# VectorE's step in another order: both gain products together, adapter work behind evictions, raw down weight fetched earlier

## The chip, the cores and the metric

The kernel runs on one core of a Trainium2 chip. The metric is the device time of one execution in microseconds (us), median over runs. One program does both layers of the reference, one after the other.

## The reference

Two layers of the same form follow each other. In each, every item of a batch of 128 (128 rows by 1024) picks one of three adapters: layer 0 by the item's own number, layer 1 by its own set of weights and the same number.

```
h = x @ W_down[r] + b_down[r]        # 1024 -> 512
h = gelu(h)
u = h @ W_up[r] + b_up[r]            # 512 -> 1024
y = x + u
y = (y - mean(y)) * rsqrt(var(y) + 1e-5)
x = y * gamma[r] + beta[r]
```

## The kernel before

**Pairs and steps.** The items are sorted by adapter (`c_ord`), so that neighbours share one, and taken two at a time. There are 65 pairs for each layer (`NP`), 130 in all (`NPH`); the second layer reads what the first has stored in `mid`. A step is the time of one pair. TensorE, VectorE, ScalarE and GpSimd each have a list of work for a step, written out by hand. The pairs overlap: in step i TensorE multiplies the down product of pair i and the up product of pair u = i-3, VectorE also transposes and splits the hidden values of pair w = i-2, and scales pair u-1.

**Accuracy.** Every fp32 operand is split in a high part (fp32r, made by ScalarE with a copy) and a low part (made by VectorE with a subtraction); a product is three matmuls of 128x128 by 128x512. A down product of a pair is 48 matmuls. The up product of two items takes seven products instead of eight (a Strassen scheme), six matmuls each, 42 in all. So a step is 90 matmuls.

**TensorE's order in a step** (`step` in its block): product 0 into bank `bX`, a quarter of the first item's down product, product 1 into `bZ`, a quarter, product 2 into `bX`, a quarter, and so on to product 6, then two quarters of the second item's. Products alternate between the banks `bX` and `bZ`. After a product VectorE adds the bank to the rows `xt` in SBUF: `onto` 1 to 3 (L834), `last_onto` 4 to 7 (L842, which also sums). Product n+1 needs the eviction of product n-1, since it goes on in that bank: product 4 waits for onto 3, product 5 for last_onto 4, product 6 for last_onto 5, and product 2 of the next step for onto 1 of that step. These are counts of the semaphore `s_v`.

**VectorE's order in a step** is given by two functions, `begin` and `end`. `end` of step i is run, then `begin` of step i+1. After `end` come the transposes of the hidden values, `transpose_h` (L809), in `begin`. In `end`, `scale` (L865) does (x - mean) * gamma for each of the two items of pair u-1; `transpose_x` (L795, in layer 1 only) turns blocks of x; `low_x` (L802), `low_h` (L824) make low parts. ScalarE then multiplies the scaled rows by the reciprocal deviation (`normal`, L633) and GpSimd adds beta (`shift`, L415), after it has raised the variance to -1/2 and multiplied it (`norm`, L405 and L408).

**Loops.** Of the steps of each layer most run in a hardware loop of six steps a turn (`steps`, `M = 6`). VectorE's and ScalarE's loop is closed between `begin` and `end`, just before onto 3.

**Change of adapter.** `when_new` reads a flag from SBUF to a register (L221) and branches; the work behind it is done when a pair has another adapter than the one before: once at the start, once in each layer and once between the layers, four times in all. `take_wd_0`, `take_wd_1`, `take_wu_0`, `take_wu_1`, `take_wu_2` split the raw weights, the high part on ScalarE and the low part on VectorE; `factors` makes the sums of blocks of the up weight that the scheme needs (L749, L751), and `take_wu_1` two more (L770, L772). Each of these operations on 128x1024 values is one VectorE instruction. `ready(p, s)` tells TensorE that the weights of a pair are there. SyncE issues all DMAs from one list; it waits in line for each.

## Time and profile before

| | |
|---|---|
| median of 3 runs | 2804.37 us (2803.05 to 2805.55) |
| the profiled execution's own time | 2803.86 us |
| its span, first to last instruction | 2802.0 us |
| mean granted clock of TensorE | 0.987 |
| TensorE busy | 2700.2 us, 96% of the span, 11714 matmuls |
| VectorE busy | 2194.5 us, 78% |
| ScalarE busy | 1702.5 us, 61% |
| GpSimd busy | 1344.6 us, 48% |

Busy time counts overlapping matmuls once. The profiled execution is 0.5 us under the median; 1.9 us of its time lie outside the span.

### The profile page before, as it was taken

To read this page: it belongs to the slowest core of one execution; us is meant where nothing else is said; L and a number is where in the kernel's file an instruction comes from. 1 tells how busy PE (TensorE), PEld (TensorE's weight loads), DVE (VectorE), ACT (ScalarE), POOL (GpSimd) and SP (SyncE) were. 2 spreads that over 40 slices of the span, in tenths; PEclk is the share of its full clock that TensorE was granted. 3 is DMA by queue.
4 is the path that set the end of the run, shared out by engine and by line. 5 is a ranking of instruction groups with operands and counts; after the bars stand their busy time and mean duration, and the time that the engine had idled before them with its cause. 6 is when DMAs were issued, how large, how long until landed. Compare 5 with 4: busy or idle time off the path is not lost.

```text
span 2802.0 us, 57328 instructions
## 1 busy us (share of the span) xinstructions
PE 2700.2 (96%) x11714; PEld 2208.4 (79%) x11714; DVE 2194.5 (78%) x3341; ACT 1702.5 (61%) x2907; POOL 1344.6 (48%) x1050
## 2 busy tenths in 40 slices
PE   6999999999999999999989999999889999999997
PEld 5788888877788888888778787878667887878785
DVE  4777776768777776777898888888888888888886
ACT  4566665666666665656656566656555566666564
POOL 0455555544555555555444444444434444444446
PEclk9999999999999999999999999999999999999998
DMA  6665666666665666666776665666676665666664
GB/s 189 199 209 199 212 209 207 212 218 219 204 223 199 212 209 207 208 204 211 217 223 202 192 222 190 214 198 201 198 210 204 211 204 189 214 201 204 197 202 145
DMA packets 365915, 573.60 MB, mean 205 GB/s; under 512 B 40960, under 2 KB 240768, under 8 KB 365440
## 3 DMA queue, kind: packets, MB, share of 16 engines
q1 hardware_dynamic: 365440, 569.61, 62.9%
q14 instruction: 463, 3.79, 0.5%
q8 instruction: 12, 0.20, 0.0%
HBM read 364.97 MB, written 204.47 MB: 203 GB/s over the span
## 4 chain that ended last, share of the span: by engine, by line
PE 73%; issue 9%; DVE 9%; DVEq 2%; ACT 2%; DMA 2%; SPq 1%; POOL 1%; ACTq 0%; POOLq 0%
PE pD L463 38%; PE bX L475 20%; PE bZ L475 15%; DVE xt L842 2%; DVEq L221 2%; DMA cbd<-in_bd 1%; DVE hl L824 1%; DVE xt L865 1%; DVE wul L743 1%; ACT pC L625 1%; DVE xl L802 1%; DVE xt L834 1%; DVE xT L795 1%; ACT xh L573 1%; SPq L269 0%
## 5 line engine op out<-in xcount | busy, mean ns | idle before, releaser
L415 POOL TENSOR_TENSOR xt<-xt,cgb 128x1024 f32<-128x1024 f32 x260 | 649.7, 2500 | 419.5 <-ACT xt L633 419.5
L463 PE MATMUL pD<-wdh,xh 128*128 128x512 f32 x2080 | 814.3, 392 | 11.1 <-ACT pD L588 10.4
L463 PE MATMUL pD<-wdl,xh 128*128 128x512 f32 x2080 | 813.2, 391 | 0.0
L463 PE MATMUL pD<-wdh,xl 128*128 128x512 f32 x2080 | 812.6, 391 | 0.0
L633 ACT ACTIVATE xt<-xt,rstd 128x1024 f32<-128x1024 f32 x260 | 298.8, 1150 | 459.2 <-POOL rstd L408 380.8
L463 PEld LDWEIGHTS pD<-wdh,xh 128*128 128x128 f32 x2080 | 393.3, 189 | 95.2 <-issue 11.2
L865 DVE SCALAR_TENSOR_TENSOR xt<-xt,nmean,cgb 128x1024 f32<-128x1024 f32 x260 | 462.3, 1778 | 0.8 <-POOLq L435 0.8
L463 PEld LDWEIGHTS pD<-wdl,xh 128*128 128x128 f32 x2080 | 393.3, 189 | 82.0
L463 PEld LDWEIGHTS pD<-wdh,xl 128*128 128x128 f32 x2080 | 392.8, 189 | 82.4
L475 PE MATMUL bX<-wuh,hh 128*128 128x512 f32 x1040 | 412.2, 396 | 45.7 <-DVE xt L834 22.4
L625 ACT ACTIVATE pC<-xt,nmean 128x512 f32<-128x512 f32 x520 | 359.8, 692 | 137.8 <-DVE nmean L850 73.4
L423 POOL TENSOR_TENSOR cs<-hT 128x256 f32<-128x256 f32 x130 | 96.6, 743 | 650.7 <-DVE hT L809 650.7
L475 PE MATMUL bX<-wuh,hl 128*128 128x512 f32 x1040 | 408.0, 392 | 0.0
L475 PE MATMUL bX<-wul,hh 128*128 128x512 f32 x1040 | 407.7, 392 | 0.0
L405 POOL TENSOR_TENSOR rstd<-var,mhalf 128x2 f32<-128x2 f32 x130 | 216.8, 1668 | 362.2 <-DVE var L857 360.6
L834 DVE TENSOR_TENSOR xt<-bX,xt 128x512 f32<-128x512 f32 x260 | 176.4, 678 | 237.1 <-PE bX L475 126.5
L615 ACT ACTIVATE hh<-cs 128x512 fp32r<-128x512 f32 x260 | 163.6, 629 | 326.1 <-PE bX L475 289.6
L475 PE MATMUL bZ<-wuh,hh 128*128 128x512 f32 x780 | 307.4, 394 | 20.0 <-DVE xt L842 18.5
L475 PE MATMUL bZ<-wul,hh 128*128 128x512 f32 x780 | 305.2, 391 | 0.0
L475 PE MATMUL bZ<-wuh,hl 128*128 128x512 f32 x780 | 304.8, 391 | 0.0
L475 PEld LDWEIGHTS bX<-wuh,hh 128*128 128x128 f32 x1040 | 196.1, 189 | 105.6 <-DVE xt L834 31.3
L802 DVE TENSOR_TENSOR xl<-xq,xh 128x1024 fp32r<-128x1024 f32 x130 | 219.7, 1690 | 40.3 <-ACT xh L573 24.7
(90 smaller groups left out, 3746.1 us busy)
## 6 DMA issues: line engine op xcount, KB each, us to landing
xq<-in_xB SPq DMA_DIRECT2D x130, 512.0 KB, 3.6
htok<-hg SPq DMA_DIRECT2D x260, 256.0 KB, 2.8
hq<-htok SPq DMA_DIRECT2D x1040, 64.0 KB, 2.2
xt<-in_x SPq DMA_DIRECT2D x130, 512.0 KB, 4.2
mid<-xt SPq DMA_DIRECT2D x130, 512.0 KB, 3.6
xq<-mid SPq DMA_DIRECT2D x520, 128.0 KB, 3.2
xt<-mid SPq DMA_DIRECT2D x130, 512.0 KB, 4.3
out<-xt SPq DMA_DIRECT2D x130, 512.0 KB, 2.7
```

Of the source, the lines that this page charges most:

```text
L221: return eng.value_load(c_new[0:1, bass.ds(p.times(1), 1)], min_val=0, max_val=1)
L405: eng.tensor_tensor(rstd[:, n:n + 2], var[:, n:n + 2], mhalf[:, 0:1].broadcast_to([128, 2]), ALU.pow)\
L415: eng.tensor_tensor(xt[:, k, :], xt[:, k, :], cgb[:, 1, :], ALU.add).then_inc(s_o, 1)
L423: eng.tensor_tensor(cs[:, 0, :], b1, b2, ALU.add).then_inc(s_S, 1)
L463: last = eng.matmul(pD[e][:, :], a[:, e, 128 * k:128 * k + 128], w[:, k, :], start=False, stop=(k == 7 and n == 2), skip_group_check=True)
L475: last = eng.matmul(bank[:, :], a[:, left, 128 * c:128 * c + 128], w[:, n, c, :], start=(start and c == 0 and m == 0), stop=(c == 1 and m ...
L615: eng.activation(dst, src, ACT.Copy).then_inc(s_hh, 1)
L625: eng.activation(junk[:, :], xt[:, u.slot(e), K * m:K * m + K], ACT.Square, bias=nmean[:, n:n + 1], accum_out=ssq[:, b, m, e:e + 1]).then_ ...
L633: eng.activation(xt[:, k, :], xt[:, k, :], ACT.Copy, scale=rstd[:, n:n + 1]).then_inc(s_z, 1)
L802: eng.tensor_tensor(xl[:, e, :], src, xh[:, e, :].bitcast(fp32), ALU.subtract).then_inc(s_xl, 1)
L834: eng.tensor_tensor(half(u, e, m), bank[:, :], half(u, e, m), ALU.add).then_inc(s_v, 1)
L865: eng.scalar_tensor_tensor(out=xt[:, k, :], in0=xt[:, k, :], scalar=nmean[:, n:n + 1], in1=cgb[:, 0, :], op0=ALU.add, op1=ALU.mult).then_i ...
```

## The change

VectorE's lists, `begin` and `end`, have the same instructions in another order, and one subtraction goes from `take_wu_1` to `factors`; two semaphore increments that nobody read fall away or move with it. SyncE's list has the raw down weight split off from its bias: the weight of pair i+2 is issued at the end of step i, the bias stays in the middle of the step before its pair, where both stood.

```diff
@@ down_weights, SyncE
                                       Wd[row, r:r + 128, :].rearrange("a (k i) n -> (a i) k n", i=32))\
                            .then_inc(s_rd[h], 16)
+
+            def down_bias(p):
+                row = adapter(p)
                 count(eng, s_sd, p + -1, 2, 2)
                 eng.dma_start(cbd[:, :], bd[row, :].broadcast_to([128, K])).then_inc(s_bd, 16)
@@ step, SyncE
                 if not (i + 1).first():
-                    when_new(eng, i + 1, down_weights)
+                    when_new(eng, i + 1, down_bias)
@@
                 if not v.first():
                     when_new(eng, v, up_biases)
+                when_new(eng, i + 2, down_weights)
@@ factors, VectorE
                 eng.wait_ge(s_sub, c * 4 + 2)
-                eng.sem_inc(s_seen, 1)
+                eng.tensor_tensor(t4, b21, t2, ALU.subtract).then_inc(s_sub, 1)
@@ take_wu_1, VectorE
                 low_wu(c * 7, 3, b22)
-                eng.tensor_tensor(t4, b21, t2, ALU.subtract).then_inc(s_sub, 1)
@@ begin, VectorE
                 transpose_h(w, 1)
-                onto(u, 1, bX[u.c % 2], 0, 0)
                 when_new(eng, i, take_wd_1)
                 ready(i, s_wd[1])
+                onto(u, 1, bX[u.c % 2], 0, 0)
@@ end, VectorE
                 scale(u + -1, 0)
+                scale(u + -1, 1)
+                low_h(w, 1)
+                last_onto(u, 4, bZ, 0, 1, 3)
                 transpose_x(i + 1, 0)
-                low_h(w, 1)
                 when_new(eng, w, take_wu_0)
                 ready(w, s_wu[0])
                 ready(w, s_cb)
-                last_onto(u, 4, bZ, 0, 1, 3)
-                scale(u + -1, 1)
                 last_onto(u, 5, X, 1, 1, 2)
                 low_x(i + 1, 0)
                 last_onto(u, 6, bZ, 0, 0, 1)
                 mean(u, 0, 6)
+                transpose_x(i + 1, 1)
                 when_new(eng, i + 1, take_wd_0)
                 ready(i + 1, s_wd[0])
-                transpose_x(i + 1, 1)
                 low_h(w, 2)
-                when_new(eng, w, take_wu_1)
-                ready(w, s_wu[1])
                 last_onto(u, 7, X, 1, 0, None)
                 mean(u, 1, 7)
                 low_h(w, 3)
+                when_new(eng, w, take_wu_1)
+                ready(w, s_wu[1])
```

VectorE, first half of `end` in the loop of layer 1, before: from the loop's closing branch and onto 3 (L834) to low_h of the second group. `xt,nmean,cgb` is scale, L795 is transpose_x.

```order
L834 TENSOR_TENSOR xt<-bX,xt 128x512
L177 ISA
L857 SCALAR_TENSOR_TENSOR var<-ssq 128x2
L177 REGISTER_ALU
L177 ISA
L865 SCALAR_TENSOR_TENSOR xt<-xt,nmean,cgb 128x1024
L214 ISA
L177 ISA
L795 STREAM_TRANSPOSE xT<-xq 128x1024
L177 REGISTER_ALU
L824 TENSOR_TENSOR hl<-cs,hh 128x512
```

The same place in the changed kernel (its lines are 4 to 5 higher: L838 is onto 3, L869 scale, L846 last_onto, L799 transpose_x).

```order
L838 TENSOR_TENSOR xt<-bX,xt 128x512
L177 ISA
L861 SCALAR_TENSOR_TENSOR var<-ssq 128x2
L177 REGISTER_ALU
L177 ISA
L869 SCALAR_TENSOR_TENSOR xt<-xt,nmean,cgb 128x1024 x2
L177 REGISTER_ALU
L828 TENSOR_TENSOR hl<-cs,hh 128x512
L177 REGISTER_ALU
L846 SCALAR_TENSOR_TENSOR xt,ys<-bZ,xt 128x512
L214 ISA
L177 ISA
```

The second scale now stands ahead of last_onto 4, and transpose_x behind it.

VectorE where one step ends and the next begins, in a step of layer 1, before: after `take_wu_1`, from last_onto 7 to the low part of the down weight's third quarter in `take_wd_1` (L724).

```order
L842 SCALAR_TENSOR_TENSOR xt,ys<-bX,xt 128x512
L850 TENSOR_SCALAR nmean<-ys 128x1
L824 TENSOR_TENSOR hl<-hT,hh 128x512
L809 STREAM_TRANSPOSE hT<-hq 128x512 x2
L834 TENSOR_TENSOR xt<-bX,xt 128x512
L221 TENSOR_LOAD c_new
L221 ISA x2
L228 COMPARE_AND_BRANCH
L240 ISA
L724 TENSOR_TENSOR wdl<-rwd,wdh 128x1024
```

The same place in the changed kernel, from the last subtraction of `take_wu_1` (L776) to onto 1 (L838).

```order
L776 TENSOR_TENSOR rwu<-twu,rwu 128x2x512
L228 UNCONDITIONAL_BRANCH
L813 STREAM_TRANSPOSE hT<-hq 128x512 x2
L221 TENSOR_LOAD c_new
L221 ISA x2
L228 COMPARE_AND_BRANCH
L240 ISA
L729 TENSOR_TENSOR wdl<-rwd,wdh 128x1024
L727 REGISTER_ALU
L729 TENSOR_TENSOR wdl<-rwd,wdh 128x1024
L228 UNCONDITIONAL_BRANCH
L838 TENSOR_TENSOR xt<-bX,xt 128x512
```

onto 1 has gone behind the down weight's second half, and `take_wu_1` from ahead of last_onto 7 to behind the low part `hl<-hT,hh`, right before the transposes.

## Rows read from the trace of the kernel before

**Rows 1.** The page: the span, and busy time of each engine.

```profile
span 2802.0 us, 57328 instructions
...
PE 2700.2 (96%) x11714; PEld 2208.4 (79%) x11714; DVE 2194.5 (78%) x3341; ACT 1702.5 (61%) x2907; POOL 1344.6 (48%) x1050
```

**Rows 2.** Stretches of time: us, busy (x instructions) by engine, granted clock, DMA.

```profile
1590.30:1715.30 125.00, 123.43 (x540) 101.06 (x540) 106.50 (x157) 76.50 (x133) 57.31 (x49) 1.00 0.64 203
1418.40:1424.40 6.00, 5.98 (x14) 4.73 (x15) 4.99 (x8) 3.60 (x5) 2.38 (x1) 0.50 1.01 345
```

**Rows 3.** Timeline of VectorE at a loop turn of layer 1: start, duration, instruction, idle before.

```profile
1710.95 0.69 DVE L834 TENSOR_TENSOR xt<-bX,xt 128x512 f32<-128x512 f32 x1 [4.68 <-PE bZ L475]
...
1711.62 1.28 DVE L865 SCALAR_TENSOR_TENSOR xt<-xt,nmean,cgb 128x1024 f32<-128x1024 f32 x1
1712.82 1.25 DVE L795 STREAM_TRANSPOSE xT<-xq 128x1024 f32<-128x1024 f32 x1
...
1714.57 0.67 DVE L842 SCALAR_TENSOR_TENSOR xt<-bZ,xt 128x512 f32<-128x512 f32 x1
1715.17 3.38 DVE L865 SCALAR_TENSOR_TENSOR xt<-xt,nmean,cgb 128x1024 f32<-128x1024 f32 x1
```

**Rows 4.** Timeline of the same turn: GpSimd's shift, and TensorE's products 5 and 6.

```profile
1715.08 2.39 POOL L415 TENSOR_TENSOR xt<-xt,cgb 128x1024 f32<-128x1024 f32 x1 [1.34 <-ACT xt L633]
...
1715.31 0.50 PE L475 MATMUL bZ<-wuh,hh 128*128 128x512 f32 x1 [0.59 <-DVE xt L842]
...
1719.22 0.50 PE L475 MATMUL bX<-wuh,hh 128*128 128x512 f32 x1 [0.89 <-DVE xt L842]
```

**Rows 5.** Timelines of VectorE's last_onto 4 and TensorE's product 5, three layer-0 turns.

```profile
246.89 0.68 DVE L842 SCALAR_TENSOR_TENSOR xt<-bZ,xt 128x512 f32<-128x512 f32 x1
248.03 0.39 PE L475 MATMUL bZ<-wuh,hh 128*128 128x512 f32 x1
...
490.11 0.39 PE L475 MATMUL bX<-wuh,hh 128*128 128x512 f32 x1
491.47 0.68 DVE L842 SCALAR_TENSOR_TENSOR xt<-bZ,xt 128x512 f32<-128x512 f32 x1
492.83 0.39 PE L475 MATMUL bZ<-wuh,hh 128*128 128x512 f32 x1
...
1119.37 0.68 DVE L842 SCALAR_TENSOR_TENSOR xt<-bZ,xt 128x512 f32<-128x512 f32 x1
1121.09 0.39 PE L475 MATMUL bZ<-wuh,hh 128*128 128x512 f32 x1
```

**Rows 6.** Timelines of VectorE and GpSimd at the program's end.

```profile
2789.72 2.47 DVE L865 SCALAR_TENSOR_TENSOR xt<-xt,nmean,cgb 128x1024 f32<-128x1024 f32 x2
2791.63 0.61 POOL L408 TENSOR_TENSOR rstd<-rstd,rooth 128x2 f32<-128x2 f32 x1
```

**Rows 7.** Timelines of ScalarE, TensorE and VectorE at changes of the down weight.

```profile
624.64 0.50 PE L475 MATMUL bX<-wuh,hh 128*128 128x512 f32 x1 [2.45 <-ACT bX L594]
...
630.30 3.48 DVE L724 TENSOR_TENSOR wdl<-rwd,wdh 128x1024 fp32r<-128x1024 f32 x2 [0.34 <-ACT wdh L521]
634.00 0.50 PE L463 MATMUL pD<-wdh,xh 128*128 128x512 f32 x1 [0.66 <-DVEq L786]
...
1999.97 0.60 ACT L588 ACTIVATE pD<-cbd 128x512 f32<-128x512 f32 x1 [3.97 <-DMA cbd<-in_bd]
2002.22 0.77 PE L475 MATMUL bX<-wuh,hh 128*128 128x512 f32 x1 [7.02 <-issue]
```

**Rows 8.** Timelines of ScalarE, VectorE and TensorE at layer 0's change of the up weight.

```profile
694.11 0.62 ACT L615 ACTIVATE hh<-hT 128x512 fp32r<-128x512 f32 x1
694.14 1.22 DVE L770 TENSOR_TENSOR twu<-rwu,twu 128x1024 f32<-128x1024 f32 x1
...
699.32 0.65 DVE L834 TENSOR_TENSOR xt<-bX,xt 128x512 f32<-128x512 f32 x1
700.03 0.50 PE L475 MATMUL bX<-wuh,hh 128*128 128x512 f32 x1 [2.94 <-DVE xt L834]
```

More of the change, by code:

```diff
@@ L356, in _ @@
             down_weights(Pair(0))
+            down_bias(Pair(0))
             def step(i):
```

## The prediction

> **What bounds the kernel now.** I read the page first. TensorE is busy 96% of a span of 2802.0 us [rows 1], so any gain has to come out of the 4% in which it waits. Its pace in a stretch without waits comes from the timeline: product 4 of a step starts at 490.11, product 5 at 492.83, and twelve matmuls lie between, 0.2267 us each [rows 5]. A step of 90 matmuls is then 20.40 us, and 130 steps are 2652 us. The other 150 us are the start, the end, the loop turns and the four changes of adapter. The view by stretches shows the turns: in layer 1 six steps from one turn to the next (540 matmuls) take 125.00 us [rows 2], which is 2.60 us more than 6 x 20.40.
>
> What waits at a turn is read in two timelines. VectorE comes to onto 3 after 4.68 us of idleness, the closing branch included [rows 3]. From there TensorE is ahead of it: product 5 waits 0.59 us and product 6 waits 0.89 us, both for an eviction (L842) [rows 4]. The reader should see what stands between: onto 3 at 1710.95, scale, transpose_x, low_h, last_onto 4 at 1714.57, and then a scale of 3.38 us instead of 1.28 [rows 3]. It lies under GpSimd's shift, 1715.08 to 1717.47 [rows 4]: the two don't run side by side. In layer 0 the same turn costs TensorE nothing. Product 5 starts 0.74 us after the start of last_onto 4 when it waits for it (1715.31 and 1714.57) [rows 3, 4]; in layer 0's turns it starts 1.14 us (first), 1.36 us and 1.72 us (last) after it [rows 5]. That leaves a reserve of 0.40 to 0.98 us, on the mean of the eight turns about 0.58.
>
> **The change part by part.**
>
> *Both scales together, layer 1's turns.* The second scale now runs 1.2 us after the first, while GpSimd still works on the variance. The end of the program shows that pair: two scales in 2.47 us, no blocking, and GpSimd's small multiplication held up to 0.61 us [rows 6]. In layer 1 the 1.2 us ahead of last_onto 4 replace transpose_x, 1.16 us from start to start [rows 3], so product 5 gains nothing. Behind it stands a transpose_x of 1.2 us in place of the scale of 3.3: last_onto 5 ends 2.1 us earlier, and product 6 no longer waits. That is its 0.89 and about 0.3 us of slow issue around it, 1.2 in all. VectorE's lateness shrinks faster in the steps behind (it loses 2.1 us of blocked time per step, and a reading of the flag after the short mean, which left it idle, is now covered by transpose_x), which I put at 0.5 us of product 4 and 5 and of small waits. So 1.7 of the 2.60 us [rows 2] come back, in nine turns: **-15.3 us**.
>
> Here the Trainium skill has a rule, SBUF — State Buffer, section "Who interferes with whom": a VectorE instruction with two SBUF inputs and a GpSimd instruction that reads SBUF exclude each other for their whole length, and the one that issued first wins. By that rule, the trace agrees: 3.38 us in place of 1.28. By it the low part of the second group (two SBUF inputs), which now follows transpose_x at once, falls under GpSimd's second shift; the rival below prices it from the rows.
>
> *Both scales together, layer 0's turns.* Layer 0 has no transpose_x. The second scale, 1.21 us, comes ahead of last_onto 4 and nothing leaves. It exceeds the reserve of 0.58 us by 0.63, and a wait of that size brings about 0.12 us of slow first matmuls (0.50 instead of 0.39 [rows 4, 5]). Eight turns: **+6.0 us**. In the plain steps VectorE has no closing branch and hence not the 4.68 us of idleness before onto 3 against it; the reserve is larger by most of that, and nothing is lost.
>
> *Down weight and bias.* The three later changes of the down weight lose first at product 0: 2.45 us at 624.64 and 7.02 us at 2002.22 (the third is between) [rows 7]. The bias, issued behind 2 MB of weight, is late (3.97 us of ScalarE's time [rows 7]), and with it the seeds of the banks. Fetched a half step earlier, the weight is out of its way, and these waits go. What is late next is `take_wd_1`. Its two subtractions take 3.48 us and end at 633.78 [rows 7]; they can't start earlier than ScalarE's copies, which follow its squares and so VectorE's last mean. onto 1 now stands behind them, so product 2 starts near 634.9, and the quarter behind it at 636.2 instead of 634.00 [rows 7]. TensorE, no longer held at product 0, idles some 5 us there, and such a pause costs again: after 5.5 us of waiting, the six microseconds from 1418.40 hold 14 matmuls at granted clock 0.50, the lower of the two levels (1.2 GHz) [rows 2], where 26 would fit. That is 2.8 us, against 1.7 after the shorter pause of before. So I put layer 0's change at +2.9 us, the one between the layers at +1.3 (VectorE comes 2 to 3 us earlier, since it waits less for ScalarE), the last at -3.0 (the wait of 7.02 leaves, and VectorE comes 5 us earlier). Together **+1.2 us**; bounds -18 (all waits gone, no new one: 12.5 of waits and 5 to 6 of lower clock) and +9 (3 us lost at each).
>
> *Up weight.* The second subtraction of `factors`, 1.22 us by its row [rows 8], now stands before onto 3 with the two others, and the second scale before last_onto 4; `take_wu_0` has left that place, so product 5 gains. But all of it is VectorE's work in a stretch in which VectorE is the bound, and what counts is when onto 1 and onto 3 of the next step are done (2.94 us of waiting at 700.03 [rows 8]). There the new order opens a hole. ScalarE's copy of the last hidden group ends at 694.73, 6.4 us after last_onto 6; before, VectorE spent that time in `take_wu_1` (its subtraction at 694.14) [rows 8]. Now the low part that needs the copy stands ahead of `take_wu_1`: VectorE idles some 2.3 us, then has three subtractions of 1.2 us still to do. Less the 1.2 us that went to `factors`, onto 1 (699.32 [rows 8]) comes 1.2 us later on that account; with the subtraction before onto 3 and a low part of the weight under GpSimd's shift I get +4.2 us in layer 0. In layer 1 the low parts gain elsewhere (no scale under the shift, less waiting for ScalarE's copies behind onto 1): +0.5 us in each of two. Together **+5.2 us**; bounds -6 and +13 (4.2 each).
>
> *Start and end.* The first change has the same hole, 2 us. In the last three steps, without down products, product 5 follows last_onto 4 at once, so 1.2 us of scale ahead of it cost, less what product 6 gains: 0.7 us each. **+4 us**; bounds 0 and +6.
>
> *SyncE.* Eight weight issues move past the load of hidden values, about 4 us of its time; those loads are needed in the next step, and a step is 20.40 us. Nothing.
>
> **The sum** is -15.3 + 6.0 + 1.2 + 5.2 + 4 = +1.1 us on the profiled execution's 2803.86 us. That is 0.5 us below the median of 2804.37, to which I apply the same difference: **2805.5 us**. About 0.2% (5.6 us) is what a measurement of this kernel can tell from no change.
>
> **The rivals.**
> - *The changes of adapter gain.* Seed waits go and the stall at product 2 is short because ScalarE, freed from the bias, brings its copies earlier. Half of the 18 us comes back and the up weight is even: -15.3 + 6.0 - 9 + 0 + 4 = -14, 2790 us. For it speaks that every wait before hangs on the late bias; against it that onto 1 is queued behind the weight. It decides if product 2 waits under 2 us. Chance 0.26.
> - *The hole in front of `take_wu_1`* costs in layer 1 what it does in layer 0: 4.2 us in place of 0.5, twice, +7.4, so 2813 us; with 3 us at each down change 2820. It ends slower than before, and decides from a hole of 1.5 us on. Chance 0.24.
> - *The low part under the second shift.* If it is held for the shift's 2.39 us [rows 4] in every step of layer 1, it eats the 2.1 us that the scale gave, the 0.5 us beside product 6's gain is lost in nine turns, +4.5, and 2810 us. The rule named above makes it so. Chance 0.12.
> - *The bias comes late anyway*, behind other traffic: the last change loses its gain, +5, 2811 us. Chance 0.05.
> - The forecast, gains in turns eaten by the rest: 0.33; its own range 2800 to 2810.
>
> **The numbers.** Of the first rival a little ends within 0.2%, of the third one half. So faster 0.27, same 0.40, slower 0.33. To leave out 2 in 10 the range goes from 2793 to 2818 us, short of the ends where all bounds of a sign meet.
>
> **What would show it.** In the changed profile: in layer 1 six steps take 123.3 us between turns, product 6 never waits there, no scale takes 3.3 us any more, but 1.28. In layer 0, TensorE waits 0.3 to 0.9 us for last_onto 4 at each turn, new. ScalarE doesn't wait for the bias after the start; product 2 waits 4 to 6 us for onto 1 at each down change, with lower clock behind it. VectorE waits about 2 us for ScalarE's copy at each up change. The forecast is wrong if product 2 hardly waits, or if layer 1's turns keep their 2.60 us.

## The result, and the profile after

The changed kernel takes **2822.24 us** (median of 6 runs, 2815.49 to 2826.75) against 2804.57 us for the kernel before on the same chip (6 runs, 2803.05 to 2805.58): a ratio of 1.0059, 95% interval 1.0049 to 1.0069. It is slower by 0.6%, above the upper end of the forecast's range, 2818. The profiled execution took 2818.81 us, its span 2817.0.

The page of the changed kernel, as [rows 1]:

```profile
span 2817.0 us, 57872 instructions
...
PE 2701.1 (96%) x11714; PEld 2213.7 (79%) x11714; DVE 2130.0 (76%) x3341; ACT 1681.8 (60%) x2907; POOL 1381.0 (49%) x1050
```

TensorE's own work has not changed (2701.1 us, was 2700.2). VectorE does the same 3341 instructions in 64.5 us less, and the kernel is slower all the same: what grew is TensorE's idle time.

**Layer 1's turns came out as forecast.** The six steps between the same two turns as in [rows 2], and a stretch behind the last change of down weight (us, busy and count by engine, granted clock, DMA):

```profile
1610.42:1733.96 123.54, 122.89 (x542) 101.18 (x541) 101.08 (x157) 75.36 (x132) 60.57 (x49) 1.00 0.63 205
2022.17:2028.17 6.00, 6.00 (x17) 4.74 (x18) 2.41 (x4) 5.52 (x12) 2.73 (x3) 0.60 0.77 258
```

123.54 us where there were 125.00, forecast 123.3. The timelines of one such turn in the changed kernel, against [rows 3, 4], and behind them a turn of layer 0, against [rows 5]:

```profile
1731.68 2.48 DVE L869 SCALAR_TENSOR_TENSOR xt<-xt,nmean,cgb 128x1024 f32<-128x1024 f32 x2
...
1734.67 0.68 DVE L846 SCALAR_TENSOR_TENSOR xt<-bZ,xt 128x512 f32<-128x512 f32 x1
...
1735.28 1.25 DVE L799 STREAM_TRANSPOSE xT<-xq 128x1024 f32<-128x1024 f32 x1
...
1733.60 0.61 POOL L413 TENSOR_TENSOR rstd<-rstd,rooth 128x2 f32<-128x2 f32 x1
1735.55 2.41 POOL L420 TENSOR_TENSOR xt<-xt,cgb 128x1024 f32<-128x1024 f32 x1 [1.34 <-ACT xt L638]
...
1735.42 0.50 PE L480 MATMUL bZ<-wuh,hh 128*128 128x512 f32 x1 [0.67 <-DVE xt L846]
...
249.66 0.50 PE L480 MATMUL bZ<-wuh,hh 128*128 128x512 f32 x1 [0.65 <-DVE xt L846]
```

The two scales stand as one pair of 2.48 us, and no scale of 3.38 us is left; GpSimd's small multiplication is held up to 0.61 us by them; the transpose runs at its own 1.25 us although the shift starts 0.27 us into it. Product 5 waits 0.67 us as before (0.59), product 6 no longer waits in any of the nine turns. In layer 0 product 5 waits 0.65 us, new.

**The first change of down weight** (raw weight issued at 606.96) in the changed kernel: timelines of SyncE's issues, VectorE and TensorE, and then a line of the view of waits for SyncE, 606 to 625 us:

```profile
606.96 4.22 SPq L269 DMA_DIRECT2D rwd<-in_Wd  x8
611.38 1.75 SPq L354 DMA_DIRECT2D hq<-htok  x4
613.25 0.36 SPq L346 DMA_DIRECT2D htok<-hg  x1
614.44 0.36 SPq L304 DMA_DIRECT2D xq<-in_xB  x1
620.64 1.74 SPq L354 DMA_DIRECT2D hq<-htok  x4
623.86 0.36 SPq L276 DMA_DIRECT2D cbd<-in_bd  x1
...
610.08 0.41 DVE L828 TENSOR_TENSOR hl<-hT,hh 128x256 fp32r<-128x256 f32 x1
619.58 0.69 DVE L838 TENSOR_TENSOR xt<-bX,xt 128x512 f32<-128x512 f32 x1 [9.09 <-issue]
...
620.33 0.50 PE L480 MATMUL bX<-wuh,hh 128*128 128x512 f32 x1 [4.10 <-DVE xt L838]
643.37 0.80 PE L480 MATMUL bX<-wuh,hh 128*128 128x512 f32 x1 [4.68 <-DVE xt L838]
...
SPq L354 <- DMA htok<-hg: 5.7, 1, 5.7
```

Three things are to be seen. VectorE stands for 9.09 us at its loop turn, for nothing that the profile names, and product 4 behind it waits 4.10 us. SyncE waits 5.7 us for the landing of a store of hidden values that was issued behind the weights, so the bias, behind the loads that follow, goes out 16.90 us after the weights. And product 2 of the next step (643.37) waits 4.68 us for onto 1, which now stands behind `take_wd_1`, where [rows 7] show no such wait.

**The last change of down weight**, the same views (VectorE's transpose waits for x blocks, ScalarE's seed for the bias):

```profile
1994.23 3.83 SPq L269 DMA_DIRECT2D rwd<-in_Wd  x8
2006.19 3.05 SPq L354 DMA_DIRECT2D hq<-htok  x4
...
2015.61 0.36 SPq L276 DMA_DIRECT2D cbd<-in_bd  x1
...
2014.78 1.26 DVE L799 STREAM_TRANSPOSE xT<-xq 128x1024 f32<-128x1024 f32 x1 [8.38 <-DMA xq<-mid]
...
2019.92 0.60 ACT L593 ACTIVATE pD<-cbd 128x512 f32<-128x512 f32 x1 [12.73 <-DMA cbd<-in_bd]
...
2022.17 0.77 PE L480 MATMUL bX<-wuh,hh 128*128 128x512 f32 x1 [12.01 <-issue]
```

ScalarE's wait for the bias has grown from 3.97 to 12.73 us, TensorE's from 7.02 to 12.01 [rows 7], and the six microseconds behind it hold 17 matmuls at granted clock 0.60 (second line above, under the six steps), where 26 would fit. Between the issue of the weights and SyncE's next issue lie 8.1 us.

**Layer 0's change of up weight**, timelines of VectorE and TensorE, against [rows 8]:

```profile
695.50 4.57 DVE L748 TENSOR_TENSOR wul<-rwu,wuh 128x1024 fp32r<-128x1024 f32 x2
699.99 2.82 DVE L765 TENSOR_TENSOR cbu<-cbu 128x512 f32<-128x512 f32 x1
703.25 0.69 DVE L846 SCALAR_TENSOR_TENSOR xt<-bX,xt 128x512 f32<-128x512 f32 x1 [0.44 <-DVE cbu L765]
...
710.63 0.69 DVE L828 TENSOR_TENSOR hl<-hT,hh 128x512 fp32r<-128x512 f32 x1 [2.21 <-ACT hh L620]
...
704.01 0.80 PE L480 MATMUL bX<-wuh,hh 128*128 128x512 f32 x1 [5.35 <-DVE xt L846]
...
725.71 0.50 PE L480 MATMUL bX<-wuh,hh 128*128 128x512 f32 x1 [3.15 <-DVE xt L838]
```

The hole of 2.21 us in front of `take_wu_1` is there as forecast (about 2). Not foreseen is the wait of product 6 (704.01) for last_onto 5, which now stands behind `take_wu_0`. The two weight subtractions there take 4.57 us and the bias's 2.82 us, where the kernel before had 2.35 and 0.68 us: with both scales early, GpSimd's two shifts (695.69 to 702.27) now fall on them.

**A ledger.** The start of product 5 of every step is compared between the two profiled executions. The table says by how much the changed kernel falls behind in each part of the program (us, changed less before):

```
part                       forecast   measured
start                        +2         +1.3
layer-0 turns                +6.0       +3.8
down change 1                +2.9       +8.5
up change 1                  +4.2       +6.2
down change 2                +1.3       +3.2
up change 2                  +0.5       -0.9
layer-1 turns               -15.3      -13.4
down change 3                -3.0       +4.3
up change 3                  +0.5       -2.8
tail                         +2         +5.7
total                        +1.1      +15.8
```

Parts end where the difference is steady; a change that overlaps a turn holds a microsecond or two of it. The last product 5 lies 15.8 us later, the profiled executions differ by 14.95, and the medians by 17.7. The three down changes give +16.0 where the forecast had +1.2: 14.8 us, as much as the ledger's whole miss of 14.7. A ledger compares one execution with one. In e6, e14, e15 and e18, which leave scales and transposes where they were, the part "layer-1 turns" comes out at -0.5 to +1.3, and in e2, e7, e8 and e16, which have SyncE's new list, at +1.2 to +5.5; e2 and e8 do the same in layer 1 and have +3.4 and +5.5. So 2 us in that row prove nothing by themselves.

### The profile page after: what moved, and what is told of

The parts are those of the page before. It is cut to its first block, busy times and chain, and to the rows that moved or that the text cites. A ratio compares the mean times of both kernels' runs of the same rounds, so it can differ in the third digit from the quotient of the medians.

```text
span 2817.0 us, 57872 instructions
## 1 busy us (share of the span) xinstructions
PE 2701.1 (96%) x11714; PEld 2213.7 (79%) x11714; DVE 2130.0 (76%) x3341; ACT 1681.8 (60%) x2907; POOL 1381.0 (49%) x1050
## 4 chain that ended last, share of the span: by engine, by line
PE 78%; issue 8%; DVE 7%; DVEq 2%; ACT 1%; SPq 1%; POOL 1%; DMA 1%; ACTq 0%; POOLq 0%
PE pD L468 41%; PE bX L480 21%; PE bZ L480 16%; DVEq L221 2%; DVE wul L748 1%; DVE xt L846 1%; DVE hl L828 1%; DVE xt L869 1%; DMA cbd<-in_bd 1%; DVE xl L806 1%; DVE xt L838 0%; POOL xt L420 0%; ACT pC L630 0%; DVE xT L799 0%; SPq L269 0%
## 5 line engine op out<-in xcount | busy, mean ns | idle before, releaser
L420 POOL TENSOR_TENSOR xt<-xt,cgb 128x1024 f32<-128x1024 f32 x260 | 627.2, 2413 | 419.1 <-ACT xt L638 419.1
L838 DVE TENSOR_TENSOR xt<-bX,xt 128x512 f32<-128x512 f32 x260 | 177.3, 682 | 228.6 <-PE bX L480 138.2
L828 DVE TENSOR_TENSOR hl<-cs,hh 128x512 fp32r<-128x512 f32 x260 | 257.3, 989 | 96.9 <-issue 95.3
L869 DVE SCALAR_TENSOR_TENSOR xt<-xt,nmean,cgb 128x1024 f32<-128x1024 f32 x260 | 321.6, 1277 | 0.4 <-POOLq L440 0.4
```

The source lines that it names most:

```text
L420: eng.tensor_tensor(xt[:, k, :], xt[:, k, :], cgb[:, 1, :], ALU.add).then_inc(s_o, 1)
L828: eng.tensor_tensor(blocks, src, high.bitcast(fp32), ALU.subtract).then_inc(s_hl, 1)
L838: eng.tensor_tensor(half(u, e, m), bank[:, :], half(u, e, m), ALU.add).then_inc(s_v, 1)
L869: eng.scalar_tensor_tensor(out=xt[:, k, :], in0=xt[:, k, :], scalar=nmean[:, n:n + 1], in1=cgb[:, 0, :], op0=ALU.add, op1=ALU.mult).then_i ...
```

## The experiments

Each ran beside the kernel before on its chip. The medians of the kernel before were 2802.88 us (the first four), 2803.17 (the next four), 2803.07 (e9 to e12), 2802.65 (e13 to e16) and 2804.71 (e17, e18). A difference between kernels of two groups also holds the difference of these medians, up to 2 us.

```
kernel                   us       ratio    95% interval
e1_vector_only          2816.61   1.0046   1.0032 to 1.0061
e2_sync_only            2815.99   1.0039   1.0025 to 1.0054
e3_onto1_first          2806.84   1.0012   1.0003 to 1.0022
e4_wu1_early            2807.39   1.0013   1.0004 to 1.0023
e5_turns_only           2800.00   0.9988   0.9978 to 0.9998
e6_bias_first           2804.53   1.0002   0.9992 to 1.0012
e7_sync_bias_mid        2807.60   1.0019   1.0010 to 1.0029
e8_sync_turn_later      2813.51   1.0036   1.0022 to 1.0050
e9_by_layer             2784.51   0.9935   0.9921 to 0.9948
e10_transpose_last      2778.05   0.9908   0.9893 to 0.9923
e11_three_undone        2802.61   1.0000   0.9991 to 1.0009
e12_layer_sync          2779.82   0.9922   0.9907 to 0.9937
e13_order_and_fetch     2775.64   0.9900   0.9883 to 0.9916
e14_onto1_behind        2807.49   1.0024   1.0014 to 1.0035
e15_up_group_behind     2810.34   1.0029   1.0018 to 1.0041
e16_sync_turn_later     2802.81   1.0002   0.9992 to 1.0012
e17_both_turns_later    2772.48   0.9885   0.9869 to 0.9902
e18_turns_control       2805.89   1.0005   0.9996 to 1.0015
```

### The two halves of the change: VectorE's order alone, SyncE's list alone

e1 is the changed kernel with SyncE's list of before, e2 the kernel before with the changed one:

```diff
-                    when_new(eng, i + 1, down_weights)   # weight and bias
+                    when_new(eng, i + 1, down_bias)
...
+                when_new(eng, i + 2, down_weights)       # end of the step
```

> The changed kernel with SyncE's list as before: the raw down weight and its bias are fetched together, one step ahead; only VectorE's order is the new one. Theory A, SyncE's move costs (the ledger of the two profiled executions has the three changes of down weight at +8.5, +3.2 and +5.4 us, 17.1 together, and everything else at about -2): 2802 to 2808 us, the step of the first down change about 6 us shorter than after, ScalarE's wait for the bias at the last two down changes back near 4 us instead of 4.0 and 12.7. Theory B, VectorE's order at the down changes (onto 1 behind the two rows of weight differences) costs it: 2815 us or more, the down changes still at +15 or more. The forecast as recorded would have it near 2805.

> The kernel before with SyncE's list as changed: the raw down weight fetched two steps ahead, at the end of the step, and the bias alone one step ahead; VectorE's order as before. Theory A (SyncE's move costs): 2814 to 2821 us, with the turn of VectorE's loop on the first down change idle for 9 us where it was 4.3, and ScalarE waiting for the bias of the last down change by 10 us or more. Theory B (VectorE's order costs): 2801 to 2806 us. If the two only cost together: both this kernel and the other below 2808.

**Measured:** 2816.61 and 2815.99 us. Theory A has e2 right and e1 wrong; theory B the reverse. Each half fits the theory that blames it: each costs 13 to 14 us by the medians, 11 to 13 by the ratios, and both together 17.7. So there were two causes to find. The ledger's three down changes are 5.0, 2.9 and 0.8 in e1 and 3.0, 0.3 and 3.7 in e2, with ScalarE waiting 11.47 us for the bias at e2's last one. That is 8.7 and 7.0, and 16.0 in the changed kernel: at the down changes the two halves add up. Where they don't, elsewhere in the program, is open. e2's profiled execution is also the fastest of its five and holds only 8.5 of its cost; 3.4 of that lie in layer 1's turns, where no adapter changes, and are not explained.

### VectorE's moves at the changes: onto 1, and the second up group

e3 and e4 each undo one move in e1, e14 and e15 make one move alone in the kernel before:

```diff
# e3, in begin (e14 is the reverse)
                 transpose_h(w, 1)
+                onto(u, 1, bX[u.c % 2], 0, 0)
                 when_new(eng, i, take_wd_1)
                 ready(i, s_wd[1])
-                onto(u, 1, bX[u.c % 2], 0, 0)
# e4, in end (e15 is the reverse, with the t4 subtraction moved to factors)
                 low_h(w, 2)
+                when_new(eng, w, take_wu_1)
+                ready(w, s_wu[1])
                 last_onto(u, 7, X, 1, 0, None)
                 mean(u, 1, 7)
                 low_h(w, 3)
-                when_new(eng, w, take_wu_1)
-                ready(w, s_wu[1])
```

> The kernel with VectorE's new order and SyncE's old list, and onto 1 (the eviction of product 1) put back ahead of the second pair of weight differences of a down change. Theory A gives this edit the price of product 6's waits at the three down changes (4.68, 2.53 and 1.70 us after, with what was there before taken off): 2 to 5 us less than the kernel with VectorE's new order alone. Theory B: 10 us or more less.

> The kernel before with onto 1 moved behind the second pair of weight differences of a down change, and nothing else. Three changes of down weight at 2 to 5 us each by the undoing in the new order (9.8 us by the times, 8.4 by the ledger's three rows): 2810 to 2814 us. If the move only costs inside the new order of the turns, where VectorE reaches this place later: 2802 to 2806 us.

> The kernel with VectorE's new order and SyncE's old list, and the second group of up-weight differences back ahead of the last eviction, where it stood before. The ledger has the three up changes at +6.15, -0.9 and -1.4 us. If the move of this group costs, the later products at the up changes (waits of 3.15, 2.07 and 2.13 us) gain: 1 to 5 us less than VectorE's new order alone. If the evictions freed by the move are worth more, it is 1 to 6 us longer.

> The kernel before with the second group of up-weight differences moved behind the last fetch of hidden values (the last low part), and the fourth difference of the factors made with the others. Undoing the first of these in the new order gave 9.2 us by the times and 6.1 by the ledger. If the price is the move's own: 2809 to 2813 us. If the forecast was right that this move is worth about nothing in the old order (the freed eviction against a later p2 and p4): 2801 to 2806 us.

**Measured:** onto 1 put back gives 9.8 us (2816.61 to 2806.84), more than theory A's 2 to 5 and just short of theory B's 10; the move alone costs 4.8 (2802.65 to 2807.49), ratio 1.0024 with 1.0014 to 1.0035, between the two spans expected for it. By the ledger the three down changes are 8.6 us longer in e1 than in e3, and 6.9 longer in e14 than before. The price is product 2's wait at each of them (the expectation of e3 calls it product 6). TensorE's timeline in e14 at the first of them:

```profile
632.50 0.79 PE L475 MATMUL bX<-wuh,hh 128*128 128x512 f32 x1 [4.59 <-DVE xt L834]
```

At the other two it waits 2.1 and 2.3 us.

The second up group put back gives 9.2 us, nearly twice the most that was expected (5), and made late alone it costs 7.7 (ratio 1.0029, 1.0018 to 1.0041). The places explain only part of it: between the profiled executions of e1 and e4 the three up changes differ by some 6, and e15's profiled execution, at 2806.15 the fastest of its seven, has +3.4 at the up changes. That the move costs is shown; where the rest of its 7.7 us lies is open.

### The turns alone

```diff
                 scale(u + -1, 0)
-                transpose_x(i + 1, 0)
+                scale(u + -1, 1)
                 low_h(w, 1)
                 when_new(eng, w, take_wu_0)
                 ...
                 last_onto(u, 4, bZ, 0, 1, 3)
-                scale(u + -1, 1)
+                transpose_x(i + 1, 0)
```

> The kernel before with one thing changed: the second row-weight product stands directly behind the first, and the transpose of x behind the eviction of product 4. Everything at a change of adapter, and SyncE's list, are as before. Theory A, the turns' part of the order is a small gain that the changes overturn: the ledger of VectorE's order alone gives start +1.2, layer-0 turns +4.3, layer-1 turns -13.8, tail +5.2, together -3.1 us, so 2797 to 2802 us against before near 2803. Theory C, the layer-1 gain comes only with the rest of the new order, or the start, the layer-0 turns and the tail eat all of it: 2803 to 2808 us.

**Measured:** 2800.00 us, ratio 0.9988: theory A. The turns' part is a gain of 3 us, made of -17.1 in layer 1, +3.5 at layer 0's turns, +4.3 in the tail, +1.3 at the start, and +6.3 at the first up change, where last_onto 4 still stands behind `take_wu_0`; the other changes give the rest, about -1. Timelines of VectorE and TensorE in e5:

```profile
684.21 4.50 DVE L743 TENSOR_TENSOR wul<-rwu,wuh 128x1024 fp32r<-128x1024 f32 x2
688.63 2.82 DVE L760 TENSOR_TENSOR cbu<-cbu 128x512 f32<-128x512 f32 x1
691.90 0.69 DVE L842 SCALAR_TENSOR_TENSOR xt<-bZ,xt 128x512 f32<-128x512 f32 x1 [0.44 <-DVE cbu L760]
...
692.65 0.80 PE L475 MATMUL bZ<-wuh,hh 128*128 128x512 f32 x1 [7.26 <-DVE xt L842]
```

In the kernel before the same two subtractions took 2.35 us and the bias's 0.68, as said; here too they lie under GpSimd's two shifts of that step (685.01 to 687.63, and 688.51 to 690.91). That is the scale's old trouble (3.38 us), handed on to the VectorE instructions that come next. The changed kernel has +6.2 at this change, e1 +6.2, e5 +6.3: the pair of scales alone is enough for all of it.

### SyncE's half: the bias and the two loop turns

e6 (kernel before) issues the bias ahead of its weights. e7 is e2 with the bias ahead of the loads:

```diff
                 store_h(v, 1)
+                if not (i + 1).first():
+                    when_new(eng, i + 1, down_bias)
                 load_blocks(i + 1, 1)
                 load_h(v, 1)
-                if not (i + 1).first():
-                    when_new(eng, i + 1, down_bias)
```

e8 is e2 with VectorE's layer-0 loop begun one step later, e16 is e7 with SyncE's layer-1 loop begun one step later, e18 the kernel before with both shifts. The number of jumps back is the same; only the steps behind which they fall are others:

```diff
-            for first in (6, NP + 5):
+            for first in firsts:      # VectorE (7, NP + 5), SyncE (6, NP + 6)
```

> The kernel before with the down bias issued ahead of the eight weight transfers of its change and not behind them. If the bias is late because it shares the queues with the weights that were issued before it, it lands some 5 us earlier, ScalarE's wait of 3.97 us at the last down change goes, and the time is 1 to 4 us less than before. If the 7.02 us of TensorE at that change are set by the hidden values or by the code of a turn, the time is that of before within 1 us.

> The kernel with SyncE's changed list and VectorE's old order (2815.99 us in its own run), with one thing more: the down bias is issued ahead of the load of the x blocks and of the hidden values, and no longer behind them. Theory A1, the bias was late because SyncE waited for the hidden values' store, which lay behind the weights in the DMA queues: the bias of the last down change is issued 10 us earlier, ScalarE's wait of 11.47 us there shrinks by 7 us or more, and the time is 4 to 8 us less (2808 to 2812 us). Theory A2, the hidden values themselves are late and the bias only came last: the wait of ScalarE goes but TensorE's 10.74 us stay within 3 us, and the time is within 3 us of the kernel without this edit.

> The kernel with SyncE's changed list and VectorE's old order (2815.99 us in its own run), with VectorE's loop over layer 0 begun one step later, so that its turns (jumps back) come one step of about 21 us later than before, and no longer just behind the issue of the weights at the first down change. Theory A3, the 8.69 us in which VectorE stands idle there are its own code, fetched behind 2 MB of weight: the idle time at the shifted turn is 3 to 5 us, the one at 614 us is gone, and that change costs 3 us less; the time is 1 to 5 us less. Rival: the idle time comes from the change itself (the evaluation of its flag, waits that the profile doesn't show), stays at 7 us or more at the same place, and the time is unchanged.

> The kernel with SyncE's changed list, VectorE's old order and the bias ahead of the loads (2807.6 us), with SyncE's layer-1 loop begun one step later, so that its jump back no longer follows the weights of the last down change. If the 18 us between the issue of those weights and that of the bias hold SyncE's own code, fetched behind 2 MB of weight, the bias is issued 3 us or more earlier, ScalarE's wait of 7.31 us shrinks by as much, and the time is 1 to 4 us less. Rival: SyncE waits there for the store of the hidden values, nothing moves, and the time is the same within 1.5 us.

> The kernel before with both loops begun one step later (VectorE's over layer 0, SyncE's over layer 1) and nothing else: the control for the runs with shifted turns. If a jump back costs extra only behind the early weights: 2801 to 2805 us. If the shifts gain by themselves (another change of adapter falls on a turn in the kernel before): 2795 to 2800 us.

**Measured.** e6: 2804.53, no difference (0.9992 to 1.0012). The bias that was late in the kernel before is not what its time hangs on: with the bias early, ScalarE waits 7.78 us for the weights where it waited 5.49, and TensorE still 5.17 us where it was 7.02.

e7: 2807.60, 8.4 us less than e2, a little better than theory A1's span. But its mechanism came out only in part. At the last down change the bias leaves 18.05 us behind the weights where it was 21.19, not 10 us sooner; ScalarE's wait there goes from 11.47 to 7.31 and TensorE's from 10.74 to 6.58, and the ledger has 4.2 us of gain. At the first down change, where the store of hidden values holds SyncE for 5.7 us in the changed kernel, e7 gains nothing (+4.2 for e2's +3.0). So the bias behind the loads is shown to cost some 4 us at the last change; the rest of the 8.4 has no place (the profiled executions differ by 5.4).

e8: 2813.51, 2.5 us less than e2, as theory A3 has it, but with intervals that overlap, and its ledger has only 1.1 us less at that change (expected 3). What is plain is where VectorE stands. VectorE's timelines at the turn in e2, and in e8 at the old place of the turn and at the new one:

```profile
614.23 0.69 DVE L839 TENSOR_TENSOR xt<-bX,xt 128x512 f32<-128x512 f32 x1 [8.69 <-issue]
...
607.26 0.69 DVE L839 TENSOR_TENSOR xt<-bX,xt 128x512 f32<-128x512 f32 x1 [1.58 <-PE bX L480]
...
638.59 0.69 DVE L839 TENSOR_TENSOR xt<-bX,xt 128x512 f32<-128x512 f32 x1 [3.31 <-issue]
```

The long idleness goes with the jump, and is 3.31 us when no weight is in flight. That it costs TensorE as much is not shown.

e16: 2802.81, 4.8 us less than e7, a little more than the 1 to 4 expected; the two intervals still overlap a little (1.0010 to 1.0029, 0.9992 to 1.0012), but the ledger has the gain in its place, the last down change at -6.2 for e7's -0.5. SyncE's issues at the last down change, first in e7:

```profile
1980.68 3.83 SPq L269 DMA_DIRECT2D rwd<-in_Wd  x8
1994.63 1.74 SPq L354 DMA_DIRECT2D hq<-htok  x4
...
1998.73 0.35 SPq L276 DMA_DIRECT2D cbd<-in_bd  x1
```

and in e16, with ScalarE's seed:

```profile
1979.46 3.83 SPq L269 DMA_DIRECT2D rwd<-in_Wd  x8
1983.49 1.74 SPq L354 DMA_DIRECT2D hq<-htok  x4
...
1987.49 0.36 SPq L276 DMA_DIRECT2D cbd<-in_bd  x1
...
1994.78 0.60 ACT L593 ACTIVATE pD<-cbd 128x512 f32<-128x512 f32 x1 [0.80 <-DMA cbd<-in_bd]
```

From the weights' last issue to the next one are 10.1 us with the jump between them (1980.68 + 3.83 to 1994.63) and 0.2 us without. The bias leaves 10.0 us sooner after the weights, ScalarE's wait goes from 7.31 to 0.80 us, and the rival is out. With the bias and this jump out of the way the early fetch is back at the time of before (ratio 1.0002). e18, the control, is at 2805.89 beside 2804.71, just above the 2801 to 2805 expected: shifting the loops gains nothing by itself.

### Both orders taken apart, and a faster kernel

e9 keeps the new order for steps that have a transpose to move, e10 moves only the transpose:

```diff
# e10, in end
                 scale(u + -1, 0)
-                transpose_x(i + 1, 0)
                 low_h(w, 1)
                 ...
                 last_onto(u, 4, bZ, 0, 1, 3)
                 scale(u + -1, 1)
+                transpose_x(i + 1, 0)
# e9: e5's order if (i + 1).exists() and (i + 1).layer() == 1, else that of before
```

> The kernel before with the turns' part of the new order (both row-weight products together, the transpose of x behind the eviction of product 4) in those steps alone whose next pair exists and is of layer 1, where there is a transpose to move; the start, layer 0 and the tail keep the old order. Theory A, the ledger of the kernel with the turns' part in all steps holds piece by piece: layer-1 turns -17.1, and its start +1.3, layer-0 turns +3.5, first up change +6.3 and tail +4.3 go: 2784 to 2790 us. Theory C, the pieces are not apart (what is gained in layer 1 is given back where the order ends): 2794 us or more.

> The kernel before with the transpose of x moved behind both the eviction of product 4 and the second row-weight product, in all steps; the two products stay apart. It separates the two halves of the new order at a turn. If the gain is the transpose's 1.75 us out from ahead of the eviction of product 4: layer 0, start and tail are as before, and the time is 2783 to 2792 us. If it is the faster pair (two products in 2.47 us where the second took 3.38 by itself under GpSimd's shift), the second product stays at 3.38 us, the transpose and the eviction of product 5 come later by it, and the time is 2796 us or more.

**Measured:** e9 2784.51 us, ratio 0.9935 (0.9921 to 0.9948), inside theory A's 2784 to 2790: the ledger's pieces are apart. e10 2778.05 us, ratio 0.9908 (0.9893 to 0.9923), 5 us below the lower end of what the first reading gave. Timelines of VectorE and GpSimd at the turn of [rows 3, 4], in e10:

```profile
1705.95 1.28 DVE L865 SCALAR_TENSOR_TENSOR xt<-xt,nmean,cgb 128x1024 f32<-128x1024 f32 x1
...
1707.75 0.68 DVE L842 SCALAR_TENSOR_TENSOR xt<-bZ,xt 128x512 f32<-128x512 f32 x1
1708.36 1.28 DVE L865 SCALAR_TENSOR_TENSOR xt<-xt,nmean,cgb 128x1024 f32<-128x1024 f32 x1
1709.55 1.25 DVE L795 STREAM_TRANSPOSE xT<-xq 128x1024 f32<-128x1024 f32 x1
...
1709.40 2.49 POOL L415 TENSOR_TENSOR xt<-xt,cgb 128x1024 f32<-128x1024 f32 x1 [1.34 <-ACT xt L633]
```

Both halves are had at once. last_onto 4 starts 2.48 us after onto 3 (1705.27), where it was 3.62 [rows 3], so product 5 no longer waits; and the second scale, although it stands by itself, takes 1.28 us, because without the transpose ahead of it it starts 1.04 us before the shift. The transpose has one input and runs under the shift at full speed.

The last four put pieces together: e11 is the changed kernel with three things mended (the bias ahead of the loads, onto 1 and the second up group back in their places), e12 is e9 and e13 is e10, each with the early fetch, e7's bias and e8's shifted loop, and e17 is e13 with e16's shift too.

> The changed kernel with three things mended at once: the down bias issued ahead of the loads of the x blocks and hidden values (priced -8.4 us by itself), onto 1 ahead of the second pair of down-weight differences (-9.8), the second group of up-weight differences ahead of the last eviction (-9.2). If the three prices are of separate places, they add up: 2791 to 2799 us, less than before. If two of them are the same slack counted twice, 2800 to 2808 us.

> The by-layer order with SyncE's two-steps-ahead fetch of the raw down weight, the bias issued ahead of the loads, and VectorE's layer-0 loop begun one step later. It asks what the early fetch is worth when its two side effects are mended. From the runs so far: the early fetch with the bias mended costs 4.4 us, of which the shifted turn gave back 2.5: 1 to 3 us more than the by-layer order. If the weight's wait of 5.49 us at the last down change was on the path, the early fetch gains instead: 1 to 4 us less than the by-layer order.

> The order with the transpose of x last (2778.05 us), with SyncE's two-steps-ahead fetch, the bias ahead of the loads, and VectorE's layer-0 loop begun one step later. In the by-layer order these three gained some 4 us, in the old order the first two cost 4.4. If the fetch gains once its side effects are mended: 2771 to 2776 us. If its gain in the by-layer order was the scatter of a few runs: 2777 to 2782 us.

> The fastest kernel so far (transpose last, early fetch, bias ahead of the loads, VectorE's layer-0 loop one step later: 2775.64 us) with SyncE's layer-1 loop begun one step later too. If its jump behind the weights costs there what it cost in the old order: 2769 to 2773 us. If it is hidden there, since neither ScalarE nor TensorE waited at that change in its profile: 2774 to 2777 us.

**Measured:** e11 2802.61, the rival's span: the three singles promise 27.4 us, together they give 19.6 (18.1 against the kernels before beside them), to the time of before. That some of their waits lie in the same changes, where one ends behind the other, is a reading and not shown. e12 2779.82, 4.7 below e9, where I had expected 1 to 3 above it; the two intervals overlap a little. e13 2775.64, in the span for a gain, with an interval that overlaps e10's. e17 **2772.48 us**, ratio 0.9885 (0.9869 to 0.9902), 32 us below before and 50 below the changed kernel. Its interval overlaps e13's; in the ledger the last down change goes from +0.3 to -7.1 between them, and the up change behind it gives back 4.1 of that (-1.7 to +2.4). So with its side effects mended the early fetch probably gains: each of the three steps (e9 to e12, e10 to e13, e13 to e17) points that way by 2 to 5 us, none by more than its own scatter. e10 and e17 are 5.6 us apart, 7.2 against their kernels before, and even their intervals overlap a little.

## Why the prediction was wrong

**The step that failed** is "SyncE. Eight weight issues move past the load of hidden values, about 4 us of its time ... Nothing", and with it "the weight is out of its way, and these waits go". The eight issues do take 4 us of SyncE's time. What I left out is that behind them 2 MB are on their way, and that three things that are not weights wait there: the store of the hidden values, on whose landing SyncE waits before all that follows in its list, the bias in the end (e7: 8.4 us by the medians, 4.2 of them found in the trace); SyncE's own jump back (e16: 4.8 us); and VectorE's (e8: 8.69 us of idleness in place of 3.31, 2.5 us by the medians, within their scatter). In e2 this half costs 13 us by the medians where the forecast had nothing, and e16, with the first two mended, costs nothing. The premise that every wait at the down changes hung on the late bias was wrong as well: e6 brings the bias early and gains nothing.

**The second step** that failed is the price of onto 1 behind `take_wd_1`. The stall was foreseen in place (4 to 6 us each; 4.68, 2.53 and 1.70 measured, so only the first in size), but was paid for with waits at product 0 that would go. The first did go (2.45 us), but product 4 of the same change waits 4.10 behind VectorE's jump; the second stayed (3.06 before, 3.27 after) and the third grew (7.02, 12.01). So the stall is a cost of its own: 4.8 us alone (e14), 9.8 in the new order (e3). With both steps the down changes came to +16.0, beyond the forecast's own bound of +9. A cost set against a gain that is itself only argued should have been held at its full size in the range.

**Terms that were right.** Layer 1's turns, -15.3 against -13.4 in the ledger and -17.1 in e5: 123.54 us for six steps, product 6 without a wait, the scale at 1.28. Layer 0's turns, +3.8 for +6.0: of eight turns one fell on the down change and one shows no wait, the other six wait 0.35 to 0.65 us. Start, +1.3 for +2.

**Terms of the wrong size.** The tail, +5.7 for +2: the last three product 5 lose 1.6, 1.1 and 3.0 us, where I had 0.7 each. The up changes, together +2.5 for +5.2, hide two errors. In layer 0 the hole was there (2.21 us), but `take_wu_0` ahead of last_onto 5 was not seen (product 6, 5.35 us), and more of its work lies under the shifts than the one low part forecast (+6.2 for +4.2). Layer 1's two changes gained 3.7 where the forecast had +1.0.

**The rivals.** "The changes of adapter gain" (0.26) is out: product 2 waits under 2 us only at the last down change, and all three lost. "The hole in front of `take_wu_1`" (0.24) named a time near the measured one, 2813 to 2820 us, by a price that did not come: the hole is 2.15 us at layer 1's first up change and 1.06 at its second, and both changes were shorter than before. Who had bet on it would have been close by luck.

The low part under the second shift (chance 0.12) came in nearly every step of layer 1, and cost nothing that can be found. VectorE's timeline in the changed kernel, with the shift at 1740.32, and the line of the grouped view:

```profile
1739.71 1.25 DVE L799 STREAM_TRANSPOSE xT<-xq 128x1024 f32<-128x1024 f32 x1
1741.39 1.88 DVE L828 TENSOR_TENSOR hl<-cs,hh 128x512 fp32r<-128x512 f32 x1 [0.43 <-issue]
...
L828 DVE TENSOR_TENSOR hl<-cs,hh 128x512 fp32r<-128x512 f32 x260 | 257.3, 989 | 96.9 <-issue 95.3 <-DVE wdl L729 0.9
```

A step has two of these low parts, and the second is the one that comes near the shift. In layer 1, 62 of its 64 take over 1 us, 1.15 us more than 0.68 on the mean; in the kernel before 3, in e5 14. There the flag of the weight is read between the mean and the transpose, as before the change; in the changed kernel the transpose comes first, and everything behind it earlier, into the shift. Layer 1's turns gained 17.1 us in e5's ledger and 13.4 here, and the 3.7 us between them look like the rival's 4.5. But e11 has the same 62 slow low parts and gains 17.6 us in these turns. So the rival's mechanism came and its price did not; what makes the 3.7 us is open, and over half of them may be scatter of the ledger.

"The bias comes late anyway, behind other traffic" had a chance of 0.05 and a price of 5 us. It is what happened at the last down change (4.3 us in place of a gain of 3.0), by another way than thought: not late in landing (from issue to landing it took 3.6, 3.7 and 4.1 us where it was 7.9, 7.8 and 8.3), but late in being issued.

## What to carry to other kernels

A large transfer that is fetched earlier is not taken out of anyone's way but put into someone else's: list every small transfer and every jump back in the microseconds behind its issue, on all engines, and ask of each who waits for it. An instruction that must not meet another engine's can be placed before it or replaced by one that is immune. Here the best order left the two scales apart and moved only the one-input transpose under the shift. Before a loss and a gain of a new order are summed, ask whether the two occur in the same steps. They didn't here (e9: 2784.51 us), and a condition that is known when the program is written kept the gain alone, for nothing at run time.

## What the runs showed of the hardware

**A jump back just behind a large transfer leaves the engine idle about twice as long.** VectorE's turn on the first down change: idle for 4.29 us in the kernel before (onto 3 at 611.33), 8.69 in e2, 9.09 in the changed kernel, whose other sixteen turns have 3.59 to 4.75. SyncE's turn behind the weights in e7: 10.1 us to its next issue, against 0.2 us in e16, where no jump lies between. In e7's other turns of layer 1 SyncE takes 7.5 to 7.8 us from the last store of a step to the next load, and 3.1 to 3.9 in the plain steps between, so an ordinary jump costs it some 4 us. The changed kernel's DMA view, 2002 to 2007 us, just before SyncE goes on at 2006.19:

```profile
q1 hardware_dynamic: 283, 0.50, 46.4%
q14 instruction: 3, 0.02, 2.1%
```

